# MetaFormer block on one core: gate weights spread by DMA, one PSUM bank for each expert of the last pair, and GpSimd taking two bands and seven additions

## The chip, the core and the metric

The kernel runs on 1 core of one Trainium2 chip. The metric is device time in microseconds (us); lower is better. The kernel before takes 136.04 us (median of 3 runs).

The engines are called as in the profile: PE (TensorE matmul) and PEld (its weight loads), DVE (VectorE), ACT (ScalarE), POOL (GpSimd), SP (SyncE, which issues most DMAs).

## What is computed

Eight images of 64 channels and 16x16 pixels go through a block of two halves, all in float32:

```python
x = x + conv_att(ln_c(x))          # first half
t = to_tokens(x)                   # (8, 256, 64)
t = t + ffn(ln_t(t))               # second half

# conv_att: qkv = 1x1 conv to 192 channels; dw = 5x5 depthwise; pw = grouped 1x1 (24 groups of 8);
#           ReLU linear attention over qkv and pw (16 heads of 8); 1x1 projection to 64; batch norm

def ffn(x, Wg, bg, W1, b1, W2, b2):            # 8 experts, hidden 256, top 2
    top_w, top_i = top_k(x @ Wg + bg, 2)
    w_dense = sum(one_hot(top_i) * softmax(top_w)[..., None])
    for e in range(8):
        h = gelu(x @ W1[e] + b1[e])
        out += w_dense[:, e:e + 1] * (h @ W2[e] + b2[e])
```

All eight experts are computed for every token; the gate weight `w_dense`, zero for six of them, multiplies the result.

## The kernel before, in words

The work is cut into `PAIRS` = 4 pairs `s` of images, each 2 x 256 tokens. Each engine runs one instruction list written out by hand; semaphores tie them together. There is no planner: the order in the program is the order on the engine. `mm` is a helper that records most matmuls, so most of them carry its line, L911; they are told apart by operands.

**Start.** PE makes the qkv products into PSUM; DVE and ACT scale them into `MS` (`scale_qkv`, `SCALED_V` = 6 on DVE, `SCALED_S` = 10 on ACT). Of the 24 convolution bands (`BAND`), DVE makes two of each head (L605), ACT the third (L413), and band number `ON_POOL` = 1 is made on POOL (L347). DVE then transposes head 0 (L667), for which all 16 scalings must be done, and PE starts the convolution: 24 bands of 5 matmuls.

**Middle.** For each pair: attention (`kv`, `qt`, `num`, `attt`, `proj`), a second layer norm, and `xt`, which turns the normalised tokens; ACT copies them to `XS` (`copy_xs`). `gate(part)` makes the gate logits of two pairs, DVE turns them into weights (`read_gates`, `gaps`, `places`, `softmax`).

**Experts.** `first_layer(s, e)`: two halves of two 128x512 matmuls each (high and low part of `W1`); each half goes to one of four PSUM banks 0, 1, 6, 7 and ACT applies GELU to it (L516). A bank can be written again when its GELU is done. `second_layer(s, e)` multiplies the hidden rows by `W2` (L1131) into `Y` banks 2 and 3, two experts to a bank. DVE weighs each result (`weigh`, L834: add `B2`, multiply by the weight `WB`, from PSUM into `WY`) and adds it up (`add_up`, L840) in `outs`. PE runs the second layers four at a time between blocks of first layers; the last eight, those of pair 3, stand in one row at the end.

**How a gate weight reaches all rows.** `tokens(s)` (L1086, L1089) turns the weights of a pair, split in two parts (`WDS`, made by DVE at L823 and L824), and the residual tokens `X2`; ACT copies both (`read_tokens`: `WT` L498, `outs` L499). Then `weights(s, ep)` spreads the weights of two experts over 128 rows with two matmuls against a 0/1 matrix `PICK`, and ACT copies the bank to `WB` (`read_weights`, L507). `MISC` = banks 5 and 4 alternate for this.

The PE order around the places that matter, word for word:

```python
            for e in range(QUAD):
                second_layer(0, e)
            xt(3)
            tokens(0)
            first_layer(0, 7)
            weights(0, 0)
            first_layer(1, 0)
```

`tokens(0)` waits there, through `wait_misc`, for ACT's copy of the tokens that `xt(3)` has just turned (`a_read[3]`, `A_XT`), since bank 4 holds them.

Of the kernel before, what the change touches and what calls it, by code (L numbers as in the profile page):

```python
# [48 lines left out]
C_ROWS = C_IOTA + E  # L49
C_END = C_ROWS + 2 * E  # L50
# [4 lines left out]
def constants():  # L55
# [11 lines left out]
    c[0:4 * E, C_ROWS:C_ROWS + 2 * E] = np.tile(np.eye(2 * E).reshape(2 * E, 2, E).transpose(0, 2, 1)  # L67
                                                 .reshape(2 * E, 2 * E), (2, 1))
# [11 lines left out]
def build(nc, x, w_qkv, w_dw, w_pw, w_proj, vectors, wg, w1, b1, w2, b2, consts, select, out):  # L80
    ctx = ExitStack()
    with ctx:
# [33 lines left out]
        PICK = sb("PICK", [128, E, 2, C], F32R)  # L116
        WT = sb("WT", [128, 2, N], F32R)
# [23 lines left out]
        WDS = sb("WDS", [128, PAIRS, 2, 2, 2, E])  # L141
# [53 lines left out]
        SCALED_V, SCALED_S = 6, 10  # L195
        ON_POOL = 1
# [4 lines left out]
        Y_BANKS, LAST_Y_BANK = (2, 3), 6  # L201
        MISC = (5, 4)
        GATE_BANKS = 1, 4
        MISC_GATES = (3,)
# [7 lines left out]
        warm_set, pick_set = sem("warm_set"), sem("pick_set")  # L212
# [24 lines left out]
        gap_ready, exp_ready, wds_ready, wt_read = sem("gap_ready"), sem("exp_ready"), sem("wds_ready"), sem("wt_read")  # L237
        misc_ready, misc_read = sem("misc_ready"), [sem("misc_read_0"), sem("misc_read_1")]
        h_ready, gelu_done, w2_done, y_read = sem("h_ready"), sem("gelu_done"), sem("w2_done"), sem("y_read")
        out_ready, stored = sem("out_ready"), sem("stored")  # L240
# [21 lines left out]
        def misc_use(s, k):  # L262

            n = (1 + E // 2) * s + k
            return n if n < MISC_GATES[0] else n + len(MISC_GATES)

        def reads_before(n):

            return sum(m % 2 == n % 2 and m not in MISC_GATES for m in range(n))

        def uses_before(n):

            return sum(m not in MISC_GATES for m in range(n))

# [18 lines left out]
        def y_bank(s, e):  # L293

            return LAST_Y_BANK if s == PAIRS - 1 and e == E - 1 else Y_BANKS[e // 2 % 2]

        def band_factors(g):

            return (band[:, g].rearrange("p d (x o) -> p (d x) o", o=I),
                    RS[:, g].rearrange("p d x -> p (d x)").unsqueeze(2).broadcast_to([128, DY * W, I]),  # L300
                    PW[:, g, :].unsqueeze(1).broadcast_to([128, DY * W, I]))

# [3 lines left out]
        def _(sp):  # L306
# [17 lines left out]
            for s in range(PAIRS):  # L324
                sp.wait_ge(out_ready, s + 1)
                sp.dma_start(out[2 * s:2 * s + 2].rearrange("b c y x -> (b c) (y x)"), outs[:, s, :]).then_inc(stored, 16)
            sp.wait_ge(stored, 16 * PAIRS)

        @block.gpsimd
        def _(pool):  # L330
# [6 lines left out]
            pool.memset(WT[:, :, :].bitcast(F32), 0.0).then_inc(pads_set, 1)  # L337
            pool.wait_ge(pads_set, 6)
# [8 lines left out]
            pool.tensor_tensor(*band_factors(ON_POOL), ALU.mult).then_inc(band_p, 1)  # L347
# [25 lines left out]

        @block.scalar
        def _(act):
# [23 lines left out]
            act.wait_ge(pads_set, 6)  # L399
# [4 lines left out]
            for j in range(6):  # L404
                scale_qkv(j, 1)
            for j in range(6, 8):
                for h in range(2):
                    scale_qkv(j, h)
# [83 lines left out]
            def read_tokens(s):  # L492

                n = misc_use(s, 0)
                act.wait_ge(misc_ready, uses_before(n) + 1)
                if s >= 2:
                    act.wait_ge(misc_ready, uses_before(misc_use(s - 1, 0)))
                act.activation(WT[0:4 * E, s % 2, :], PS[0:4 * E, MISC[n % 2], N:2 * N], ACT.Copy).then_inc(wt_read, 1)  # L498
                act.activation(outs[:, s, :], PS[:, MISC[n % 2], 0:N], ACT.Copy).then_inc(misc_read[n % 2], 1)  # L499

            def read_weights(s, ep):

                n = misc_use(s, 1 + ep)
                act.wait_ge(misc_ready, uses_before(n) + 1)
                if s >= 2:
                    act.wait_ge(y_read, E * (s - 2) + 2 * ep + 2)
                act.activation(WB[:, s % 2, 2 * ep:2 * ep + 2, :].rearrange("p e n -> p (e n)"),  # L507
                               PS[:, MISC[n % 2], :], ACT.Copy).then_inc(misc_read[n % 2], 1)

# [46 lines left out]
            high(3)  # L556
            copy_xs(3)
            read_tokens(0)
            gelu(0, 7)
            read_weights(0, 0)  # L560
            gelu(1, 0)
            read_weights(0, 1)
            gelu(1, 1)
            gelu(1, 2)
            read_weights(0, 2)
            gelu(1, 3)
            read_weights(0, 3)
            gelu(1, 4)
            read_tokens(1)
            gelu(1, 5)  # L570
            gelu(1, 6)
            read_weights(1, 0)
            gelu(1, 7)
            read_weights(1, 1)
            for s in (2, 3):
                gelu(s, 0)
                gelu(s, 1)
                read_weights(s - 1, 2)
                gelu(s, 2)
                read_weights(s - 1, 3)  # L580
                gelu(s, 3)
                read_tokens(s)
                if s == 2:
                    gelu(s, 4)
                    gelu(s, 5)
                    read_weights(s, 0)
                    gelu(s, 6)
                    read_weights(s, 1)
                    gelu(s, 7)
            for k in range(QUAD):  # L590
                gelu(PAIRS - 1, QUAD + k)
                read_weights(PAIRS - 1, k)

        @block.vector
        def _(dve):
# [68 lines left out]
            for h in range(8):  # L664
# [4 lines left out]
                else:  # L669
                    dve.transpose(qp[:, 3 * h:3 * h + 3], head(h)).then_inc(qp_ready, 1)  # L670
                if h > 0:
# [131 lines left out]
            def softmax(part):  # L803
# [13 lines left out]
                for b in range(2):  # L817
                    i = dve.tensor_tensor(WDN[:, pairs, :, b, :], O1.rearrange("p (s b h) e -> p b s h e", b=2, h=2)[:, b],
                                          O2.rearrange("p (s b h) e -> p b s h e", b=2, h=2)[:, b], ALU.add)
                link(i)  # L820
                whole = WDN[:, pairs].rearrange("p s h b e -> p (s h) (b e)")
                parts = WDS[:, pairs].rearrange("p s h k b e -> p k (s h) (b e)")
                link(dve.tensor_copy(parts[:, 0].bitcast(F32R), whole))  # L823
                dve.tensor_tensor(parts[:, 1].bitcast(F32R), whole, parts[:, 0], ALU.subtract).then_inc(wds_ready, 1)  # L824

            def combine(s, ep):

                for n in (misc_use(s, 0), misc_use(s, 1 + ep)):
                    dve.wait_ge(misc_read[n % 2], reads_before(n) + 1)
# [3 lines left out]
                def weigh(e):  # L833
                    dve.scalar_tensor_tensor(out=WY[:, e % 2, :], in0=PS[:, y_bank(s, e), N * (e % 2):N * (e % 2) + N],  # L834
# [11 lines left out]
                if y_bank(s, 2 * ep) == y_bank(s, 2 * ep + 1):  # L846
# [51 lines left out]
            combine(0, 0)  # L898
            read_gates(1)
            combine(0, 1)  # L900
            gaps(1)
            places(1)
            combine(0, 2)
            softmax(1)
            for n in range(3, PAIRS * E // 2):
# [3 lines left out]
        def _(pe):  # L909
# [143 lines left out]
            def gate(part):  # L1053
# [7 lines left out]
                for n in MISC_GATES if part == 1 else ():  # L1061
                    pe.wait_ge(misc_read[n % 2], reads_before(n))
# [7 lines left out]
            def wait_misc(n):  # L1070

                if n in (MISC_GATES[0] + 1, MISC_GATES[-1] + 1, MISC_GATES[-1] + 2) and n not in MISC_GATES:
                    pe.wait_ge(gate_read, 2)
                if n >= 2:
                    pe.wait_ge(misc_read[n % 2], reads_before(n))
                else:
                    pe.wait_ge(b_read[PAIRS - 1], B_PROJ)
                    pe.wait_ge(a_read[PAIRS - 1], A_XT)

            def tokens(s):  # L1080

                n = misc_use(s, 0)
# [177 lines left out]
```

## Time and profile before

| | us |
|---|---|
| runs (3) | 136.04 median, 135.68 to 136.23 |
| profiled execution | 136.38 |
| its span, first to last instruction | 134.6 |
| PE busy | 126.6 (94%) |
| ACT busy | 95.2 (71%) |
| DVE busy | 85.4 (63%) |
| POOL busy | 22.3 (17%) |

The profiled execution takes 1.78 us more than its span, and 0.34 us more than the median of the runs. The chain that ended last (followed back from the last instruction) is 90% PE, 4% DVE and 2% ACT.

### The profile page before, as it was taken

Reading aid. Unit: us, or ns where it says so; the run is one execution under the profiler, and the core shown is the slowest. Engines: PE = TensorE matmul, PEld = TensorE weight load, DVE = VectorE, ACT = ScalarE, POOL = GpSimd, SP = SyncE. Lnnn points to the kernel's source line nnn. Section 1 sums busy time; section 2 is a strip of 40 time slices with the busy share of each in tenths; the row PEclk is TensorE's granted clock in tenths of the full one; section 3 lists DMA queues with packets and bytes.
Section 4 is the critical chain, followed back from the end, with each engine's and each line's share of the span. In section 5 each row is a group of like instructions: output and inputs, shape, how many; then the busy total and the mean of one; then the engine's idle time right before and its main releaser. Section 6 shows DMA issues by size and latency. Waiting matters only on the chain.

```text
span 134.6 us, 2740 instructions
## 1 busy us (share of the span) xinstructions
PE 126.6 (94%) x954; PEld 102.9 (76%) x954; DVE 85.4 (63%) x252; ACT 95.2 (71%) x220; POOL 22.3 (17%) x22
## 2 busy tenths in 40 slices
PE   7999699999999999979999899999999999999970
PEld 7498699999998899957875786776867668677640
DVE  0528899999976986974693099946318072270793
ACT  3357999999984928359994797493984939759400
POOL 4005999300000000230720004000000000000000
PEclk9999999999999999999999999999999999999999
DMA  4779300000000000000000000010000100001001
GB/s 123 227 167 215 100 2 0 0 5 0 0 2 0 5 0 0 5 0 0 0 0 0 5 2 0 2 39 5 0 0 0 39 5 0 0 0 39 0 7 39
DMA packets 3655, 3.48 MB, mean 26 GB/s; under 512 B 978, under 2 KB 3258, under 8 KB 3642
## 3 DMA queue, kind: packets, MB, share of 16 engines
q1 hardware_dynamic: 3264, 3.09, 9.0%
q10 hardware_dynamic: 378, 0.22, 0.6%
q8 instruction: 8, 0.13, 0.4%
q14 instruction: 5, 0.04, 0.1%
HBM read 2.78 MB, written 0.52 MB: 25 GB/s over the span
## 4 chain that ended last, share of the span: by engine, by line
PE 90%; DVE 4%; ACT 2%; issue 2%; POOL 0%; DVEq 0%; ACTq 0%; POOLq 0%
PE PS L911 61%; PE PS L1131 20%; PE PS L1012 3%; PE PS L1049 2%; ACT MS L390 1%; PE PS L1018 1%; DVE SQ L834 1%; PE PS L1035 1%; DVE XP L840 1%; PE PS L1086 1%; PE PS L1089 1%; ACT KR L428 1%; DVE BAND L605 1%; ACT XS L490 0%; DVE MS L657 0%
## 5 line engine op out<-in xcount | busy, mean ns | idle before, releaser
L516 ACT ACTIVATE MS<-PS,B 128x512 f32<-128x512 f32 x48 | 30.1, 694 | 12.3 <-PE PS L911 12.2
L834 DVE SCALAR_TENSOR_TENSOR SQ<-PS,B,BAND 128x256 f32<-128x256 f32 x32 | 14.1, 479 | 28.6 <-ACT XP L499 10.1
L911 PE MATMUL PS<-QP,BAND 128*128 128x120 f32 (+2 forms) x240 | 27.0, 275 | 0.8 <-DVE QP L667 0.8
L911 PEld LDWEIGHTS PS<-QP,BAND 128*128 128x128 f32 x240 | 26.9, 192 | 1.0 <-issue 1.0
L911 PE MATMUL PS<-XS,W1H 128*128 128x512 f32 x64 | 26.7, 416 | 0.7 <-ACT XS L490 0.7
L911 PE MATMUL PS<-XS,W1L 128*128 128x512 f32 x64 | 25.3, 395 | 0.0
L1131 PE MATMUL PS<-MS,W 128*64 128x256 f32 x192 | 22.3, 383 | 0.0
L1131 PEld LDWEIGHTS PS<-MS,W 128*64 128x64 f32 x192 | 13.2, 137 | 7.4 <-issue 0.4
L413 ACT ACTIVATE BAND<-RS,PW 128x80 f32<-128x80 f32 x64 | 17.2, 434 | 0.0
L911 PEld LDWEIGHTS PS<-XS,W1H 128*128 128x128 f32 x64 | 12.1, 189 | 5.3 <-issue 2.1
L840 DVE TENSOR_TENSOR XP<-XP,SQ 128x256 f32<-128x256 f32 x32 | 13.4, 420 | 0.6
L911 PEld LDWEIGHTS PS<-XS,W1L 128*128 128x128 f32 x64 | 12.1, 189 | 1.6
L605 DVE TENSOR_TENSOR BAND<-RS,PW 128x640 f32<-128x640 f32 x15 | 11.6, 809 | 0.0
L360 POOL TENSOR_TENSOR SM<-SM,HALF 128x4 f32<-128x4 f32 x4 | 4.2, 1046 | 38.3 <-DVE SM L755 38.3
L516 ACT ACTIVATE BAND<-PS,B 128x512 f32<-128x512 f32 x16 | 10.2, 706 | 0.0
L507 ACT ACTIVATE BAND<-PS 128x512 f32<-128x512 f32 x16 | 9.8, 615 | 0.0
L1131 PE MATMUL PS<-BAND,W 128*64 128x256 f32 x64 | 7.6, 379 | 0.0
L911 PEld LDWEIGHTS PS<-WT,PICK 128*128 128x128 f32 x32 | 5.9, 188 | 1.5
L911 PE MATMUL PS<-WT,PICK 128*128 128x256 f32 x32 | 6.4, 282 | 0.0
L1131 PEld LDWEIGHTS PS<-BAND,W 128*64 128x64 f32 x64 | 4.6, 137 | 2.3
L670 DVE STREAM_TRANSPOSE QP<-MS 128x384 f32<-128x384 f32 x7 | 6.0, 859 | 0.0
L474 ACT ACTIVATE BAND<-PS 128x512 f32<-128x512 f32 x4 | 2.4, 606 | 5.0 <-PE PS L1035 5.0
(120 smaller groups left out, 172.6 us busy)
## 6 DMA issues: line engine op xcount, KB each, us to landing
W<-in_w_dram SPq DMA_DIRECT2D x3, 512.0 KB, 6.8
X<-in_x_dram SPq DMA_DIRECT2D x2, 256.0 KB, 3.2
out_dram<-XP SPq DMA_DIRECT2D x4, 128.0 KB, 1.7
VEC<-in_vectors_dram SPq DMA_DIRECT2D x1, 132.0 KB, 3.1
SELF<-in_select_dram ACTq DMA_DIRECT2D x1, 100.8 KB
WQ<-in_w_qkv_dram SPq DMA_DIRECT2D x2, 48.0 KB, 3.4
PW<-in_w_pw_dram SPq DMA_DIRECT2D x1, 96.0 KB, 3.1
CST<-in_consts_dram SPq DMA_DIRECT2D x1, 85.0 KB, 3.3
```

The source lines that it names most:

```text
L360: pool.tensor_tensor(SM[:, s, 1, :], SM[:, s, 0, :], HALF[:, 0:TILES], ALU.pow).then_inc(r2_ready, 1)
L413: i = act.activation(band[:, g].rearrange("p d (x o) -> p o (d x)", o=I)[:, o], RS[:, g].rearrange("p d x -> p (d x)"), ACT.Copy, scale=PW ...
L507: act.activation(WB[:, s % 2, 2 * ep:2 * ep + 2, :].rearrange("p e n -> p (e n)"), PS[:, MISC[n % 2], :], ACT.Copy).then_inc(misc_read[n % ...
L516: act.activation(hidden(n), PS[:, h_bank(n), :], ACT.Gelu, bias=B1[:, k:k + 1]).then_inc(gelu_done, 1)
L605: dve.tensor_tensor(*band_factors(g), ALU.mult).then_inc(band_v, 1)
L670: dve.transpose(qp[:, 3 * h:3 * h + 3], head(h)).then_inc(qp_ready, 1)
L834: dve.scalar_tensor_tensor(out=WY[:, e % 2, :], in0=PS[:, y_bank(s, e), N * (e % 2):N * (e % 2) + N], scalar=B2[:, e:e + 1], in1=WB[:, s % ...
L840: i = dve.tensor_tensor(outs[:, s, :], outs[:, s, :], WY[:, e % 2, :], ALU.add)
L911: return pe.matmul(PS[0:parts, bank, cols[0]:cols[1]], lhsT, rhs, start=start, stop=stop)
L1012: i = pe.matmul(PS[rows, CHAIN_BANK[s], 0:2 * KW], KR[:, s, r, rows], VM[:, s, half, r].rearrange("p b v -> p (b v)"), start=r == 0, stop= ...
L1049: i = pe.transpose(PS[:, CHAIN_BANK[s], 128 * t:128 * t + 128], XHL[:, s % 2, t].rearrange("p k c -> p (k c)"), IDT)
L1131: i = pe.matmul(PS[C * b:C * b + C, y_bank(s, e), N * (e % 2):N * (e % 2) + N], W2[:, KC * e + k, :], hidden(KC * (E * s + e) + k)[:, N * ...
```

## The change

It has four parts.

1. **Gate weights by transfers.** `PICK`, the 32 matmuls against it and ACT's 16 copies to `WB` go. ACT copies the turned weights to `WT` (16x256, no split in two parts), SP writes `WT` to a buffer in DRAM (`spread`), waits for that, and reads it back with four DMAs for each pair, each of 4 experts for 64 rows, 256 KB. DVE waits on `wb_in` for each four experts.
2. **Y banks.** Pairs 0 to 2 use banks 2, 3, 4 in turn, two experts to a bank. In the last pair each expert has its own bank (`LAST_Y_BANKS`). `tokens(s)` always uses bank 5.
3. **Adding.** In the last pair POOL adds up experts 0 to 6 in `outs`, DVE only weighs, and adds the last.
4. **Start.** POOL makes bands 0 and 1; the scalings are shared 8 and 8; DVE no longer makes band 0.

With these the hand-written orders change too: `tokens(0)` stands ahead of `xt(3)`; ACT reads the tokens of pair 1 after `gelu(1, 3)` instead of after `gelu(1, 4)`; DVE reads the second gates ahead of `combine(0, 0)` instead of behind it.

```diff
-        SCALED_V, SCALED_S = 6, 10
-        ON_POOL = 1
+        SCALED_V, SCALED_S = 8, 8
+        ON_POOL = 2
-        Y_BANKS, LAST_Y_BANK = (2, 3), 6
-        MISC = (5, 4)
+        Y_BANKS, LAST_Y_BANKS = (2, 3, 4), (2, 3, 4, 5, 0, 1, 6, 7)
+        TOKEN_BANK = 5
...
+            def spread_weights(s):
+                sp.wait_ge(wt_read, s + 1)
+                sp.dma_start(spread[s], WT[:, s % 2, :]).then_inc(wt_out, 16)
+                sp.wait_ge(wt_out, 16 * (s + 1))
+                if s >= 2:
+                    sp.wait_ge(y_read, E * (s - 1))
+                for quad in range(2):
+                    for b in range(2):
+                        rows = slice(E * b + QUAD * quad, E * b + QUAD * quad + QUAD)
+                        sp.dma_start(WB[C * b:C * b + C, s % 2, QUAD * quad:QUAD * quad + QUAD, :],
+                                     spread[s, rows, :].unsqueeze(0).broadcast_to([C, QUAD, N]))\
+                            .then_inc(wb_in[s % 2][quad], 16)
...
+            spread_weights(0)
+            spread_weights(1)
+            store(0)
+            spread_weights(2)
+            store(1)
+            spread_weights(3)
+            store(2)
+            store(3)
...
+            for g in range(ON_POOL):
+                pool.tensor_tensor(*band_factors(g), ALU.mult).then_inc(band_p, 1)
...
+            s = PAIRS - 1
+            pool.wait_ge(tokens_read, PAIRS)
+            for e in range(E - 1):
+                pool.wait_ge(y_read, E * s + e + 1)
+                if e >= 1:
+                    pool.wait_ge(added, e)
+                pool.tensor_tensor(outs[:, s, :], outs[:, s, :], WY[:, e % 2, :], ALU.add).then_inc(added, 1)
...
-            copy_xs(3)
             read_tokens(0)
+            copy_xs(3)
             gelu(0, 7)
...
+            for e in range(4):
+                gelu(1, e)
             read_tokens(1)
+            for e in range(4, E):
+                gelu(1, e)
...
+                dve.wait_ge(wb_in[s % 2][2 * ep // QUAD], 32 * (s // 2 + 1))
...
                     for e in range(2 * ep, 2 * ep + 2):
                         dve.wait_ge(w2_done, E * s + e + 1)
+                        if e >= 2:
+                            dve.wait_ge(added, e - 1)
                         weigh(e)
-                        add_up(e)
+                    if ep == E // 2 - 1:
+                        dve.wait_ge(added, E - 1)
+                        add_up(E - 1)
...
             def second_layer(s, e):
                 pe.wait_ge(gelu_done, KC * (E * s + e) + KC)
-                if E * s + e >= 4:
-                    pe.wait_ge(y_read, E * s + 2 * (e // 2) - 2)
+                bank, at, end = y_part(s, e)
+                if s == PAIRS - 1:
+                    if bank in Y_BANKS:
+                        pe.wait_ge(y_read, E * s - 4 + 2 * Y_BANKS.index(bank))
+                    elif bank == TOKEN_BANK:
+                        pe.wait_ge(tokens_read, PAIRS)
+                    else:
+                        pe.wait_ge(gelu_done, KC * E * PAIRS - 4 + H_MANY.index(bank) + 1)
+                elif E * s + e >= 6:
+                    pe.wait_ge(y_read, E * s + 2 * (e // 2) - 4)
+                elif e >= 4:
+                    pe.wait_ge(gate_read, 2)
```

How the order moves on PE, right behind the second layers of pair 0's first four experts (the first row of each piece; CST,BAND x4 is `xt(3)`, the pair of x2 rows is `tokens(0)`, the W1H and W1L rows are first layers). Before:

```order
L1131 MATMUL PS<-MS,W 64x256 x16
L1049 MATMUL PS<-CST,BAND 128x128 x4
L1086 MATMUL PS<-CST,WDS 32x128 x2
L1089 MATMUL PS<-CST,BAND 128x128 x2
L911 MATMUL PS<-XS,W1H 128x512
L911 MATMUL PS<-XS,W1L 128x512
L911 MATMUL PS<-XS,W1H 128x512
L911 MATMUL PS<-XS,W1L 128x512
L911 MATMUL PS<-WT,PICK 128x256 x2
```

And in the changed kernel (its line numbers are its own):

```order
L1096 MATMUL PS<-MS,W 64x256 x16
L1052 MATMUL PS<-CST,WDN 16x128 x2
L1055 MATMUL PS<-CST,BAND 128x128 x2
L1025 MATMUL PS<-CST,BAND 128x128 x4
L887 MATMUL PS<-XS,W1H 128x512
L887 MATMUL PS<-XS,W1L 128x512
L887 MATMUL PS<-XS,W1H 128x512
L887 MATMUL PS<-XS,W1L 128x512
L887 MATMUL PS<-XS,W1H 128x512
```

`tokens(0)` has moved ahead of `xt(3)`, and the two matmuls against `PICK` behind each first layer are gone.

On ACT, around the tokens of pair 1 (MS,B and BAND,B rows of L516 are GELUs, two to an expert; L507 is `read_weights`, L498 and L499 are `read_tokens(1)`). Before:

```order
L507 ACTIVATE BAND<-PS 128x512
L516 ACTIVATE MS<-PS,B 128x512 x2
L507 ACTIVATE BAND<-PS 128x512
L516 ACTIVATE MS<-PS,B 128x512 x2
L498 ACTIVATE WT<-PS 32x256
L499 ACTIVATE XP<-PS 128x256
L516 ACTIVATE MS<-PS,B 128x512 x2
```

In the changed kernel, where L515 is the GELU and L506 and L507 are `read_tokens`:

```order
L515 ACTIVATE BAND<-PS,B 128x512 x2
L515 ACTIVATE MS<-PS,B 128x512 x8
L506 ACTIVATE WT<-PS 16x256
L507 ACTIVATE XP<-PS 128x256
L515 ACTIVATE MS<-PS,B 128x512 x4
L515 ACTIVATE BAND<-PS,B 128x512 x4
```

The GELUs of expert 4 of pair 1 stood ahead of the two token copies and now stand behind them; the copies to `WB` are gone.

On DVE, the last rows of the program, pair 3 (SQ is `weigh`, XP is `add_up`). Before:

```order
L834 SCALAR_TENSOR_TENSOR SQ<-PS,B,BAND 128x256 x2
L840 TENSOR_TENSOR XP<-XP,SQ 128x256 x2
L834 SCALAR_TENSOR_TENSOR SQ<-PS,B,BAND 128x256
L840 TENSOR_TENSOR XP<-XP,SQ 128x256
L834 SCALAR_TENSOR_TENSOR SQ<-PS,B,BAND 128x256
L840 TENSOR_TENSOR XP<-XP,SQ 128x256
```

In the changed kernel, the last of pair 2 and then pair 3:

```order
L807 SCALAR_TENSOR_TENSOR SQ<-PS,B,BAND 128x256 x2
L813 TENSOR_TENSOR XP<-XP,SQ 128x256 x2
L807 SCALAR_TENSOR_TENSOR SQ<-PS,B,BAND 128x256 x2
L813 TENSOR_TENSOR XP<-XP,SQ 128x256 x2
L807 SCALAR_TENSOR_TENSOR SQ<-PS,B,BAND 128x256 x8
L813 TENSOR_TENSOR XP<-XP,SQ 128x256
```

Eight weighings now follow each other with one addition behind them; the seven others stand on POOL.

## Rows read from the trace of the kernel before

**Rows 1.** The page, parts 1 and 2: busy us; granted clock in tenths.

```profile
PE 126.6 (94%) x954; PEld 102.9 (76%) x954; DVE 85.4 (63%) x252; ACT 95.2 (71%) x220; POOL 22.3 (17%) x22
...
PEclk9999999999999999999999999999999999999999
```

**Rows 2.** The chain that ended last, start of the convolution: start us, us, what.

```profile
14.35 0.62 issue
...
15.63 25.92 PE PS L911 x230
```

**Rows 3.** Timelines of DVE, ACT and POOL up to 28 us: start us, us.

```profile
11.57 2.04 DVE L632 TENSOR_SCALAR MS<-PS,R 128x192 f32<-128x192 f32 x6
27.99 0.18 DVE L681 TENSOR_TENSOR INV<-INV,VEC 128x64 f32<-128x64 f32 x1
11.63 3.25 ACT L390 ACTIVATE MS<-PS,R 128x192 f32<-128x192 f32 x10 [0.79 <-PE PS L911]
11.57 1.29 POOL L347 TENSOR_TENSOR BAND<-RS,PW 128x640 f32<-128x640 f32 x1 [4.36 <-DVE RS L636]
12.82 0.38 POOL L350 TENSOR_SCALAR INV<-VEC 128x64 f32<-128x64 f32 x1
18.71 5.94 POOL L354 TENSOR_TENSOR INV<-INV,HALF 128x32 f32<-128x32 f32 x1
```

**Rows 4.** The chain that ended last: around `tokens(0)`; a block of four first layers.

```profile
73.69 0.73 issue
...
75.02 6.49 PE PS L911 x36
...
102.00 4.41 PE PS L911 x20
```

**Rows 5.** Timeline of PE in the last first layers.

```profile
119.44 0.40 PE L911 MATMUL PS<-WT,PICK 128*128 128x256 f32 x2
...
119.67 0.40 PE L911 MATMUL PS<-XS,W1H 128*128 128x512 f32 x1
...
119.91 0.40 PE L911 MATMUL PS<-XS,W1L 128*128 128x512 f32 x1
```

**Rows 6.** Timeline of ACT: token copies, and a block of four GELUs.

```profile
75.06 0.37 ACT L498 ACTIVATE WT<-PS 32x256 fp32r<-32x256 f32 x1 [0.73 <-PE PS L1089]
...
75.60 1.23 ACT L516 ACTIVATE BAND<-PS,B 128x512 f32<-128x512 f32 x2
...
102.70 2.43 ACT L516 ACTIVATE MS<-PS,B 128x512 f32<-128x512 f32 x4 [2.30 <-PE PS L911]
105.00 0.62 ACT L507 ACTIVATE BAND<-PS 128x512 f32<-128x512 f32 x1
```

**Rows 7.** Timeline of DVE: second gates, `gaps(1)` up to `combine(0, 2)`.

```profile
79.22 0.22 DVE L778 TENSOR_TENSOR BAND<-PS,VEC 128x64 f32<-128x64 f32 x1
...
81.44 0.65 DVE L787 MAX8 BAND<-BAND 128x8 f32<-128x8 f32 x8
...
83.83 0.88 DVE L834 SCALAR_TENSOR_TENSOR SQ<-PS,B,BAND 128x256 f32<-128x256 f32 x2
```

**Rows 8.** Timelines of PE and DVE at the end.

```profile
128.51 1.90 PE L1131 MATMUL PS<-BAND,W 128*64 128x256 f32 x16
...
131.51 0.48 DVE L834 SCALAR_TENSOR_TENSOR SQ<-PS,B,BAND 128x256 f32<-128x256 f32 x1
132.03 0.42 DVE L840 TENSOR_TENSOR XP<-XP,SQ 128x256 f32<-128x256 f32 x1
```

**Rows 9.** DMA: issue of X on SP, its readers on DVE, landing of the stores.

```profile
0.72 0.38 SPq L307 DMA_DIRECT2D X<-in_x_dram  x1
...
3.72 0.60 DVE L610 COPY XP<-X 128x512 f32<-128x512 f32 x1 [3.72 <-DMA X<-in_x_dram]
4.62 0.61 DVE L610 COPY XP<-X 128x512 f32<-128x512 f32 x1 [0.30 <-DMA X<-in_x_dram]
...
out_dram<-XP SPq DMA_DIRECT2D x4, 128.0 KB, 1.7
```

More of the change, by code:

```diff
@@ L260, in head @@
             return MS[:, :, :].rearrange("p j (q h i) -> p h q j i", q=3, i=I)[:, h]
[L262 to L273, printed above, removed]
         def h_bank(n):
@@ L291, in masked_v, with y_part @@
                     PAR[:, b:b + 1])
-        def y_bank(s, e):
-            return LAST_Y_BANK if s == PAIRS - 1 and e == E - 1 else Y_BANKS[e // 2 % 2]
+        def y_part(s, e):
+            bank, at = (LAST_Y_BANKS[e], 0) if s == PAIRS - 1 else (Y_BANKS[(E * s + e) // 2 % 3], N * (e % 2))
+            return bank, at, at + N
         def band_factors(g):
@@ L403, in _ @@
             act.wait_ge(r1_ready, 1)
-            for j in range(6):
+            for j in range(SCALED_S):
                 scale_qkv(j, 1)
-            for j in range(6, 8):
-                for h in range(2):
-                    scale_qkv(j, h)
             def bands(g):
@@ L897, in _ @@
             dve.wait_ge(b2_in, 32)
-            combine(0, 0)
             read_gates(1)
-            combine(0, 1)
             gaps(1)
             places(1)
-            combine(0, 2)
+            combine(0, 0)
+            combine(0, 1)
             softmax(1)
-            for n in range(3, PAIRS * E // 2):
+            for n in range(2, PAIRS * E // 2):
                 combine(*divmod(n, E // 2))
@@ L1068, in gate, with tokens @@
                 i.then_inc(gate_ready, 1)
[L1070 to L1075, printed above, removed]
-                else:
[L1077 to L1082, printed above, removed]
-                wait_misc(n)
-                pe.wait_ge(wds_ready, s // OF_PART + 1)
+            def tokens(s):
+                if s == 0:
+                    pe.wait_ge(b_read[PAIRS - 1], B_PROJ)
+                else:
+                    pe.wait_ge(tokens_read, s)
+                pe.wait_ge(wdn_ready, 2 * (s // OF_PART) + 2)
                 for half in range(2):
-                    pe.transpose(PS[0:4 * E, MISC[n % 2], N + 128 * half:N + 128 * half + 128],
-                                 WDS[:, s, half].rearrange("p k b e -> p (k b e)"), IDT)
+                    pe.transpose(PS[0:2 * E, TOKEN_BANK, N + 128 * half:N + 128 * half + 128],
+                                 WDN[:, s, half].rearrange("p b e -> p (b e)"), IDT)
                 for half in range(2):
-                    i = pe.transpose(PS[:, MISC[n % 2], 128 * half:128 * half + 128],
+                    i = pe.transpose(PS[:, TOKEN_BANK, 128 * half:128 * half + 128],
                                      X2[:, 2 * s + half].rearrange("p b c -> p (b c)"), IDT)
-                i.then_inc(misc_ready, 1)
-            def weights(s, ep):
-                n = misc_use(s, 1 + ep)
-                wait_misc(n)
-                pe.wait_ge(wt_read, s + 1)
-                pe.wait_ge(pick_set, 1)
-                for e in range(2):
-                    i = mm(MISC[n % 2], (N * e, N * e + N), PICK[:, 2 * ep + e].rearrange("p b c -> p (b c)"),
-                           WT[:, s % 2, :], True, True)
-                i.then_inc(misc_ready, 1)
+                i.then_inc(turned, 1)
             def first_layer(s, e):
@@ L1122, in second_layer @@
                 pe.wait_ge(gelu_done, KC * (E * s + e) + KC)
[L1123 to L1124 removed]
+                bank, at, end = y_part(s, e)
+                if s == PAIRS - 1:
[9 more added lines that the diff above has]
+                    pe.wait_ge(gate_read, 2)
                 else:
@@ L1130, in second_layer @@
                 for k, b in ((0, 0), (0, 1), (1, 1), (1, 0)):
-                    i = pe.matmul(PS[C * b:C * b + C, y_bank(s, e), N * (e % 2):N * (e % 2) + N],
+                    i = pe.matmul(PS[C * b:C * b + C, bank, at:end],
                                   W2[:, KC * e + k, :], hidden(KC * (E * s + e) + k)[:, N * b:N * b + N],
@@ L1171, in _ @@
                 second_layer(0, e)
+            tokens(0)
             xt(3)
-            tokens(0)
             first_layer(0, 7)
-            weights(0, 0)
             first_layer(1, 0)
-            weights(0, 1)
-            first_layer(1, 1)
             gate(1)
-            first_layer(1, 2)
-            weights(0, 2)
-            first_layer(1, 3)
-            weights(0, 3)
+            for e in range(1, QUAD):
+                first_layer(1, e)
             for e in range(QUAD, E):
@@ L1187, in _ @@
             tokens(1)
-            first_layer(1, 5)
-            first_layer(1, 6)
-            weights(1, 0)
-            first_layer(1, 7)
-            weights(1, 1)
+            for e in range(5, E):
+                first_layer(1, e)
             for e in range(QUAD):
@@ L1197, in _ @@
                 first_layer(s, 1)
-                weights(s - 1, 2)
+                tokens(s)
                 first_layer(s, 2)
-                weights(s - 1, 3)
                 first_layer(s, 3)
-                tokens(s)
                 for e in range(QUAD, E):
                     second_layer(s - 1, e)
+                for e in range(QUAD, E):
+                    first_layer(s, e)
                 if s == 2:
-                    first_layer(s, 4)
-                    first_layer(s, 5)
-                    weights(s, 0)
-                    first_layer(s, 6)
-                    weights(s, 1)
-                    first_layer(s, 7)
                     for e in range(QUAD):
                         second_layer(s, e)
-            for k in range(QUAD):
-                first_layer(PAIRS - 1, QUAD + k)
-                weights(PAIRS - 1, k)
             for e in range(E):
```

120 lines of the change are left out of this document (34 added, 86 removed).

## The prediction

> **What bounds the kernel now.** I read the page first: PE is busy 94% of the span and its granted clock is full in every slice [rows 1]. Then the chain that ended last, in order of time: it lies on PE but for three places. One is the start, where PE waits for the first transpose on DVE, and DVE in turn waited 0.62 us with nothing of its own to do [rows 2]; ACT's ten scalings end at 11.63 + 3.25 = 14.88, DVE's six at 13.61, so it waited for ACT [rows 3]. The second is a hole of 0.73 us in front of `tokens(0)` [rows 4], which waits for ACT's copy of the tokens just turned. The third is the tail on DVE: PE ends at 128.51 + 1.90 = 130.41, DVE at 132.03 + 0.42 = 132.45 [rows 8]. So an instruction taken off PE is worth its pitch, one taken off ACT or DVE nothing in itself.
>
> **The change part by part.** Call the end of PE's last matmul P; all times are on the clock of the span before.
>
> *Start.* DVE's six scalings take 2.04, a pitch of 0.33; eight end at about 11.57 + 2.04 + 0.66 = 14.27. ACT's ten give a pitch of 0.31, eight end near 14.25 [rows 3]. The transposes then start near 14.4 instead of 14.97 (14.35 + 0.62 [rows 2]). POOL's two bands of 1.29 end at 12.86 and 14.15 [rows 3], ahead of the first matmul; POOL reads and writes other tiles than the scalings do, as band 1 did before. The convolution follows without a gap for 25.92 us [rows 2], so its start moves everything: **-0.6**. Hidden: POOL's powers end at 24.65 + 1.3 = 25.9, ahead of their first reader at 27.99 - 0.6 = 27.4 [rows 3]. Were DVE to slow POOL's second band by half, PE would reach it (a band later, 1.08 us by 25.92 / 24) still in time.
>
> *`tokens(0)` ahead of `xt(3)`.* It no longer uses bank 4, so it doesn't wait for ACT's copy; that copy is next needed by `gate(1)`, two first layers on (1.9 us), and it takes ACT about 0.5. The way to 75.02 [rows 4] loses the 0.73 and perhaps 0.15 of the restart: **-0.8** (0.7 to 0.9).
>
> *The 32 `PICK` matmuls.* Two of them start at 119.44 and the next first-layer matmul at 119.67 [rows 5]: 0.234 a pair (their listed durations overlap), 16 pairs: **-3.75**. What could hide this gain is ACT, whose GELUs free the banks. Its pitch is (105.00 - 102.70) / 4 = 0.575 [rows 6] against PE's 2 x 0.235 = 0.47 a half [rows 5]. In a block of eight halves the first GELU starts 0.70 after the block (102.70 [rows 6] against 102.00 [rows 4]), the fourth ends at 0.70 + 2.30 + 0.1 = 3.1, and PE wants its bank at 7 x 0.47 = 3.3: no stall, by 0.2. Between blocks lie 3.6 us of second layers, and ACT catches up, the more so since it lost 16 copies.
>
> *ACT reads the tokens of pair 1 ahead of `gelu(1, 4)`.* Here a new wait arises. Count from the start of `first_layer(1, 4)`. PE needs 0.94 for it, 0.6 for `tokens(1)` (75.02 less 73.69 + 0.73 [rows 4]); ACT then copies for 75.60 - 75.06 = 0.54 [rows 6] and starts the first GELU at about 2.15, where before it ran ahead of the copies. GELU k ends at 2.15 + 0.1 + 0.575 (k + 1). PE wants the bank of the first GELU at 0.94 + 0.6 + 0.94 = 2.5, has it at 2.85, and that of the fourth at 4.6 instead of 3.9: **+0.75**, once. Pairs 2 and 3 read their tokens behind `gelu(s, 1)`, when PE has long turned them. Bounds 0 and 0.9.
>
> *Transfers.* Nobody waits for them if they land in time; the first pair is the tightest. `WT` is there at 75.06 + 0.37 = 75.43 [rows 6]; it comes 0.6 earlier by the start, 0.73 by the hole and 0.6 because `xt(3)`, four transposes like `tokens(0)`, now stands behind: 73.5. A store of 128 KB lands 1.7 after issue; X's first 256 KB are there 3.72 - 0.72 = 3.0 after issue and the next 0.9 later [rows 9]. So the first four experts (512 KB) land at 73.5 + 1.7 + 3.9 + 0.1 = 79.2, the other four at 81.0. `first_layer(0, 7)` starts at 75.02 - 0.6 - 0.8 = 73.6; it, the next and `gate(1)` (6.49 less five experts of 0.94 and four pairs of 0.234 [rows 4, 5]: 0.85) end near 76.3, and DVE is through with second gates, gaps and places 0.5 (two instructions of 0.22) + (83.83 - 81.44) = 2.9 later [rows 7], at 79.3. So `combine(0, 0)` starts at 79.3 and its two weighings end at 80.2 (0.88 [rows 7]). PE needs them for bank 2 at `second_layer(0, 6)`: the block starts at 75.02 + 6.49 = 81.51 less 0.6, 0.8 and four `PICK` pairs (0.94), 79.15, and its third expert 1.8 later, at 80.95. Slack 0.7: **0**. Later pairs have it easier: the weights of pair 1 land about 6 us ahead of the bank that would stop PE, those of pair 3 some 3 us ahead of the first weighing. SP's stores stand behind transfers, but each waits for sums that are complete before the next weights are wanted.
>
> [...]
>
> *Tail.* Before, DVE spends 0.94 on each expert (weigh and add), more than PE's 0.9, and ends at P + 2.04. Now weigh 7 starts at P + 0.1 and ends at P + 0.58. The addition 6 on POOL: its weighing ends at P - 0.32; a 128x64 instruction of POOL takes 0.38 and one of 128x640 1.29 [rows 3], on the line between them 128x256 is 0.68, with both as bounds; it ends at P + 0.46, DVE's last addition at P + 1.05: **-1.0**. POOL's pitch of 0.68 + 0.1 stays under PE's 0.9, so no queue forms. The separate banks take PE's waits for weighings away, of which it had none in this stretch, and the store behind the last addition is as before.
>
> [...]
>
> **Sum.** -0.6 - 0.8 - 3.75 + 0.75 - 1.0 = -5.4. The profiled execution took 136.38, so its like would take 131.0; the median of the runs lies 0.34 lower, which gives 130.7.
>
> **The rivals.**
> - *A, the sum as it stands*: 130.7; chance 0.60.
> - *B, the first weights come late.* For: a DRAM buffer is written and then read by 64 rows at once, which nothing in this trace does; the slack is 0.7. Against: X moves at 0.9 a 256 KB beside other loads. At half that rate the first four land at 81.0, and PE stands 1.0: 131.7, up to 132.5 if the write takes 0.8 longer too. Chance 0.15.
> - *C, POOL's additions queue.* The first weighing ends at P - 5.7; seven additions of pitch p, then DVE's, end at P - 5.1 + 7p. From p = 0.9 on they lengthen the tail, at 1.02 all of its gain is gone (131.7), at 1.29, the upper bound, + 0.1 it would be 134.3. For: POOL's start behind a semaphore isn't shown at this pace. Against: the line between two rows. Chance 0.10.
> - *D, the wait at pair 1's tokens doesn't arise*, since a GELU slips in or PE's halves are slower: 130.0. Chance 0.08.
> - *E, slower than before.* One mechanism: the weights of pair 0 land so late that PE loses 5.4 at `second_layer(0, 6)`. That needs them at 79.2 + 0.7 + 5.4 = 85.3 or later, 11.8 after `WT` where I count 5.7, as would be if 64 rows reading the same 4 KB went one after another (about 50 GB/s). With every pair hit the same way the time would be 137 or more. Against: the wide loads of constants at the start come from one row of DRAM too and hold nobody up. Chance 0.04, and 0.03 for a loss between B and this that ends within 0.5% of before.
>
> **Range and chances.** A measurement of this kernel tells about 0.5% from no change. A to D reach from 130.0 to 132.5; with 0.2 for the spread of the runs below, the range is 129.8 to 132.4. Faster 0.94, same 0.02, slower 0.04.
>
> **What would show each step.** The first convolution matmul near 15.05. No hole in front of `tokens(0)`. Blocks of four first layers of 3.75 to 3.95 us. A hole of 0.4 in front of `first_layer(1, 6)`, and short ones after it. DVE's first weighing near 79.3, held by places and not by a DMA. POOL's seven additions 0.9 apart, 0.7 each; DVE's last addition 1.05 behind PE's last matmul. Wrong if PE waits at `second_layer(0, 6)` for DVE, if the additions run closer than 0.9 to their own length, or if the GELUs' pitch grows and holds every block.

## The result

The changed kernel takes 131.15 us (median of 4 runs, 130.39 to 136.53), the kernel before 136.11 (median of 4). In some executions of every kernel here the time is some microseconds longer at a mean granted clock near 0.97; the ratios and, but where a mean clock is given, the times below leave them out, and four of the profiles (tokens0_behind_xt3, more_room, two_late, more_room_two_late) are such ones, with PE's granted clock at 0.50 from about 10 to 17 us and the convolution starting near 18.8 instead of 15, so that only stretches behind that point are read there. The ratio is 0.962 (95% interval 0.957 to 0.968): 5.1 us faster.

The profiled execution took 131.66 (136.38 before), its span is 129.8. The page of the changed kernel, parts 1, 2 and 6 (busy us; granted clock; DMAs with KB and us to landing):

```profile
PE 123.1 (95%) x922; PEld 98.2 (76%) x922; DVE 81.9 (63%) x242; ACT 85.8 (66%) x201; POOL 27.7 (21%) x29
...
PEclk9999999999999999999999999999999999999998
...
BAND<-spread_dram SPq DMA_DIRECT2D x16, 256.0 KB, 4.7
```

PE is as full as before [rows 1] over a shorter span, and the granted clock held (0.995 in the mean, 1.00 up to 128 us, behind PE's last matmul). The chain that ended last, of the changed kernel, beside [rows 2, 4]:

```profile
15.02 25.92 PE PS L887 x230
...
72.47 0.32 PE PS L1052 x2
72.78 0.22 PE PS L1055 x2
73.00 0.44 PE PS L1025 x4
73.44 5.56 PE PS L887 x28
79.00 1.88 PE PS L1096 x16
80.88 0.12 issue
81.00 1.95 PE PS L1096 x16
82.94 1.12 PE PS L887 x4
...
85.08 0.67 ACT MS L515
85.75 0.14 issue
85.89 2.35 PE PS L887 x8
88.24 3.60 PE PS L1096 x32
...
99.79 3.92 PE PS L887 x16
...
119.17 2.77 PE PS L1096 x23
```

The hole of 0.73 [rows 4] is gone; a block of four first layers takes 3.92 where it took 4.41. Two waits remain among the experts: a short one at 80.9, and one where the chain leaves PE for ACT's GELU up to 85.75. The timelines of DVE, SP and ACT in the changed kernel show what they are:

```profile
79.97 0.88 DVE L807 SCALAR_TENSOR_TENSOR SQ<-PS,B,BAND 128x256 f32<-128x256 f32 x2 [0.90 <-DMA BAND<-spread_dram]
...
73.44 0.35 SPq L312 DMA_DIRECT2D spread_dram<-WT  x1
74.89 2.38 SPq L319 DMA_DIRECT2D BAND<-spread_dram  x4
...
84.82 0.36 ACT L507 ACTIVATE XP<-PS 128x256 f32<-128x256 f32 x1
85.08 2.37 ACT L515 ACTIVATE MS<-PS,B 128x512 f32<-128x512 f32 x4
```

DVE had been through with its places at 79.07 and waited 0.90 for the transfer. ACT's GELUs of expert 4 of pair 1 start at 85.08, behind the token copies, and PE goes on behind the first of them. And the timelines at the end, beside [rows 8]:

```profile
120.97 5.95 POOL L388 TENSOR_TENSOR XP<-XP,SQ 128x256 f32<-128x256 f32 x7 [41.68 <-DVE SQ L807]
...
124.33 1.90 PE L1096 MATMUL PS<-BAND,W 128*64 128x256 f32 x16
...
126.28 0.48 DVE L807 SCALAR_TENSOR_TENSOR SQ<-PS,B,BAND 128x256 f32<-128x256 f32 x1 [0.21 <-PE PS L1096]
126.95 0.42 DVE L813 TENSOR_TENSOR XP<-XP,SQ 128x256 f32<-128x256 f32 x1 [0.18 <-POOL XP L388]
```

PE ends at 126.23, DVE at 127.37, 1.14 behind it instead of 2.04; the last 0.18 of DVE's wait is for POOL.

### The profile page after: what moved, and what is told of

Same layout as the page of the kernel before. It is cut to its first block, busy times and chain, and to the rows that moved or that the text cites. A ratio compares the mean times of both kernels' runs of the same rounds, so it can differ in the third digit from the quotient of the medians.

```text
span 129.8 us, 2655 instructions
## 1 busy us (share of the span) xinstructions
PE 123.1 (95%) x922; PEld 98.2 (76%) x922; DVE 81.9 (63%) x242; ACT 85.8 (66%) x201; POOL 27.7 (21%) x29
## 4 chain that ended last, share of the span: by engine, by line
PE 86%; DVE 3%; DMA 3%; POOL 2%; ACT 2%; issue 1%; POOLq 1%; DVEq 0%; ACTq 0%
PE PS L887 57%; PE PS L1096 19%; PE PS L988 3%; DMA CST<-in_consts_dram 3%; POOL XP L388 2%; DVE MS L608 2%; PE PS L994 1%; PE PS L1025 1%; PE PS L1011 1%; PE PS L947 1%; PE PS L1052 1%; PE PS L1055 1%; POOLq L79 1%; ACT KR L437 1%; ACT MS L515 1%
## 5 line engine op out<-in xcount | busy, mean ns | idle before, releaser
L515 ACT ACTIVATE MS<-PS,B 128x512 f32<-128x512 f32 x48 | 29.2, 681 | 12.0 <-PE PS L887 12.0
L388 POOL TENSOR_TENSOR XP<-XP,SQ 128x256 f32<-128x256 f32 x7 | 5.1, 727 | 42.5 <-DVE SQ L807 41.7
L813 DVE TENSOR_TENSOR XP<-XP,SQ 128x256 f32<-128x256 f32 x25 | 10.5, 420 | 0.6 <-POOL XP L388 0.2
L581 DVE TENSOR_TENSOR BAND<-RS,PW 128x640 f32<-128x640 f32 x14 | 10.7, 801 | 0.0
L515 ACT ACTIVATE BAND<-PS,B 128x512 f32<-128x512 f32 x16 | 9.8, 695 | 0.0
L483 ACT ACTIVATE BAND<-PS 128x512 f32<-128x512 f32 x4 | 2.4, 604 | 5.0 <-PE PS L1011 5.0
L506 ACT ACTIVATE WT<-PS 16x256 f32<-16x256 f32 x4 | 1.5, 365 | 6.1 <-PE PS L1055 6.1
L360 POOL TENSOR_TENSOR INV<-INV,HALF 128x32 f32<-128x32 f32 x1 | 5.5, 5457 | 0.1
```

The lines of the kernel that those rows point to most:

```text
L360: pool.tensor_tensor(INV[:, 1, 0:C // 2], INV[:, 0, 0:C // 2], HALF[:, 0:C // 2], ALU.pow).then_inc(inv_ready, 1)
L388: pool.tensor_tensor(outs[:, s, :], outs[:, s, :], WY[:, e % 2, :], ALU.add).then_inc(added, 1)
L515: act.activation(hidden(n), PS[:, h_bank(n), :], ACT.Gelu, bias=B1[:, k:k + 1]).then_inc(gelu_done, 1)
L581: dve.tensor_tensor(*band_factors(g), ALU.mult).then_inc(band_v, 1)
L813: i = dve.tensor_tensor(outs[:, s, :], outs[:, s, :], WY[:, e % 2, :], ALU.add)
```

## The experiments

All kernels are edits of the changed kernel, and their times are compared with those of after_again, its repetition. Two stretches of PE are read in each trace: from the first row of `second_layer(0, 4)` to the first of `second_layer(0, 6)`, 1.78 us where nothing is waited for, and from there to `second_layer(1, 0)`.

**after_again.** No edit. 

> The changed kernel once more, as the measure for the three beside it. 130.4 to 131.2 us; PE's last matmul 1.1 to 1.2 us ahead of DVE's last addition.

Measured 130.81 to 131.50 (130.81, 130.92, 130.95, 131.50); ratio to before 0.9645 (0.962 to 0.967). Stretches 1.93 and 7.17; DVE ends 1.15 behind PE. The wait for the first weights was 0.15 here, 0.29 in the profile above (2.07).

**tail_on_dve.**

```diff
-                        if e >= 2:
-                            dve.wait_ge(added, e - 1)
                         weigh(e)
-                    if ep == E // 2 - 1:
-                        dve.wait_ge(added, E - 1)
-                        add_up(E - 1)
+                        add_up(e)
```

POOL's seven additions are left out. 

> The changed kernel with POOL's seven additions back on DVE (own banks kept). Theory (POOL takes 0.42 us an expert off DVE, which is slower than PE by 0.04 to 0.1 us an expert): DVE ends about 2.0 us behind PE's last matmul instead of 1.14, so 0.8 to 0.9 us slower than the changed kernel. Rival (the separate banks bring the gain, POOL's pitch of 0.87 us eats its own): within 0.3 us of the changed kernel.

Measured 131.25, 132.39, 132.48 (two at a mean clock of 0.992); these times alone don't tell 0.3 from 0.8, the trace does. Its chain that ended last:

```profile
118.23 7.09 PE PS L1085 x63
...
126.84 0.42 DVE XP L806
```

PE's last matmul ends at 125.29, DVE at 127.26: 1.97 behind, where it is 1.15 in after_again. The theory holds: the last pair's own banks alone bring 0.07 at the tail (2.04 before), POOL brings 0.82. The first stretch is 1.78 in this trace: here PE did not wait for the first weights at all, though nothing in that part was edited.

**tokens1_behind_gelu4.**

```diff
-            for e in range(4):
+            for e in range(5):
                 gelu(1, e)
             read_tokens(1)
-            for e in range(4, E):
+            for e in range(5, E):
                 gelu(1, e)
```

> ACT reads the tokens of pair 1 behind the GELUs of expert 4 instead of ahead of them. Theory: the hole in front of first_layer(1, 6) and the short ones after it go, 0.6 to 0.75 us faster than the changed kernel, and the weights of pair 1 land 1 us later, which nobody waits for at the end. Rival: the hole moves to a later wait (the weights of pair 1 come later) and the time stays within 0.2 us.

Measured 130.59, 131.42, 131.66. The chain that ended last in its trace:

```profile
79.90 0.89 DVE SQ L807 x2
80.78 0.14 issue
80.92 1.95 PE PS L1096 x16
82.87 1.12 PE PS L887 x4
83.99 0.22 PE PS L1052 x2
84.20 0.22 PE PS L1055 x2
84.42 2.83 PE PS L887 x12
87.25 3.60 PE PS L1096 x32
```

The three first layers behind the tokens run without a break, and the second stretch is 6.26 instead of 7.17: the hole of 0.9 is gone, as the theory has it. The first stretch, ahead of the edit, was 2.29, a wait of 0.51 for the first weights. The times of the runs alone don't decide; two ran at a mean clock of 0.987.

**tokens0_behind_xt3.** `xt(3)` ahead of `tokens(0)`, which waits for `a_read[3]`, and `copy_xs(3)` ahead of `read_tokens(0)`.

```diff
+            xt(3)
             tokens(0)
-            xt(3)
             first_layer(0, 7)
```

> tokens(0) back behind xt(3) with its wait for the copied tokens, ACT's order as before. Theory: PE stands 0.7 us there, and the first weights come 0.7 + 0.6 us later, so the weighings that PE wants at second_layer(0, 6) end 0.6 us later against PE's own schedule and add up to 0.6 us there: 0.8 to 1.4 us slower than the changed kernel. Rival (another wait hides behind it): within 0.3 us.

Measured 133.84, 133.99, 134.49: 3.0 slower than the changed kernel, more than twice what was expected. The order's own hole is there as computed (0.73 of idle ahead of `tokens(0)`). The rest is at the first weights; PE and SP in its trace, and the stretch from 88 to 90 us (columns as in the table of transfers_late below):

```profile
87.49 2.86 PE L1097 MATMUL PS<-BAND,W 128*64 128x256 f32 x16 [2.02 <-DVE SQ L807]
...
78.48 0.35 SPq L312 DMA_DIRECT2D spread_dram<-WT  x1
80.91 2.38 SPq L319 DMA_DIRECT2D BAND<-spread_dram  x4
...
88.00:90.00 2.00, 2.00 (x14) 1.18 (x10) 1.90 (x6) 0.00 (x0) 0.00 (x0) 0.59 0.00 0
```

The first stretch is 3.96, a wait of 2.18, and the 16 matmuls behind it took 2.86 instead of 1.90, at a granted clock of 0.59. The wait adds up from the traces: 0.29 as in the changed kernel; 0.44, since SP starts the write 5.05 ahead of `second_layer(0, 4)` instead of 5.49, which is the order's part; 0.98, since the write of `WT` took 2.43 from issue to the next issue instead of 1.45; and 0.48, since the first weighing came 5.56 behind the first read's issue instead of 5.08. The three timed runs had a mean clock of 0.998 to 1.000, so they did not pay for the clock; whether they had so slow a write is not shown, though their 3.0 need a wait near 2 us there.

**start_as_before.** `SCALED_V, SCALED_S = 6, 10`, `ON_POOL = 1`, band 0 on DVE, as in the kernel before. 

> The changed kernel with the start of before: scalings 6 and 10, band 0 on DVE, band 1 alone on POOL. Theory: the convolution starts at 15.6 instead of 15.0 on the clock of the span, 0.6 us slower than the changed kernel (131.3 to 131.7). Rival: a later wait absorbs it, within 0.2 us.

Measured 131.76, 131.82 (against 130.81 to 131.50). From DVE's first scaling to the convolution 4.10 (11.05 to 15.15) against 3.44 (10.93 to 14.37) in after_again: 0.66, and nothing absorbs it; the runs are 0.74 slower in the mean.

**no_transfers.** POOL fills `WB` with 0.125 once the convolution is done; SP spreads nothing.

```diff
+            pool.wait_ge(conv_moved, 9)
+            pool.memset(WB[:, :, :, :].rearrange("p s e n -> p (s e n)"), 0.125).then_inc(wb_set, 1)
-                dve.wait_ge(wb_in[s % 2][2 * ep // QUAD], 32 * (s // 2 + 1))
+                dve.wait_ge(wb_set, 1)
```

> The gate weights are left out: POOL fills WB once with a constant, SP moves nothing between the experts (the sums are therefore not the reference's). Theory (transfers are hidden but for the first pair): 0.1 to 0.3 us faster than the changed kernel, the wait at second_layer(0, 6) gone. Rival (the traffic slows engines or the stores): 0.5 us faster or more, with shorter matmuls, GELUs or a faster last store.

Measured 130.79, 131.07, 131.11, 131.12; the changed kernel 130.81 to 131.50. First stretch 1.78, second 7.15 as with transfers. So 4 MB of traffic costs PE its wait for the first weights and nothing else that shows in the time; GELUs (681 and 682 ns in the mean) and first-layer matmuls (422 and 423 ns for W1H) keep their lengths. The stores do not: their median from issue to landing is 2.3 in the changed kernel (1.8 to 3.1 in its edits with transfers) and 1.7 without, as before. The first three are waited for by nobody, and the span ends 2.4 behind DVE's last addition in both traces.

**transfers_late.** Four transfers of 256 KB ahead of pair 0's, into the slot that pair 1 uses later.

```diff
+                if s == 0:
+                    for n in range(4):
+                        sp.dma_start(WB[C * (n % 2):C * (n % 2) + C, 1, 4 * (n // 2):4 * (n // 2) + 4, :],
+                                     spread[0, 0:QUAD, :].unsqueeze(0).broadcast_to([C, QUAD, N])).then_inc(idle_in, 16)
+                if s == 1:
+                    sp.wait_ge(idle_in, 16 * 4)
```

> Four idle transfers of 256 KB ahead of the four of pair 0. Theory (slack at second_layer(0, 6) is used up): at about 1.15 us each the first weights land 4.6 us later and PE stands there 4.5 us: 4 to 4.8 us slower than the changed kernel, near 135.2. Rival (there is slack of a microsecond or more, or DVE catches up ahead of PE): under 3.5 us slower.

Measured 138.28, 138.56, 139.78, 139.93: 8 slower, where 4 to 4.8 were expected. PE in its trace, and the table by stretch (busy us of PE, PEld, DVE, ACT, POOL, then granted clock, DMA share, GB/s):

```profile
86.94 3.68 PE L1103 MATMUL PS<-BAND,W 128*64 128x256 f32 x16 [5.61 <-DVE SQ L814]
...
82.00:84.00 2.00, 0.00 (x0) 0.00 (x0) 0.00 (x0) 0.00 (x0) 0.00 (x0) 1.00 1.04 234
84.00:86.00 2.00, 0.00 (x0) 0.00 (x0) 0.09 (x1) 0.00 (x0) 0.00 (x0) 0.72 0.75 166
86.00:88.00 2.00, 1.06 (x6) 0.78 (x8) 1.93 (x5) 0.00 (x0) 0.00 (x0) 0.50 0.03 10
88.00:90.00 2.00, 2.00 (x14) 1.17 (x10) 1.83 (x8) 0.00 (x0) 0.00 (x0) 0.50 0.00 0
90.00:92.00 2.00, 2.00 (x8) 1.18 (x5) 1.93 (x8) 0.00 (x0) 0.00 (x0) 0.57 0.00 0
```

The hole is 5.8. The granted clock fell inside it, near 84.9 by the 0.72 of that row, and was at 0.50 until near 91.7 by the 0.57 of the last one: the 16 matmuls took 3.68 instead of 1.90. So there was no slack, as the theory says, and a long hole has a second price. Each idle transfer moved the first weights by 1.4 (first issue to first weighing 10.57 against 5.08).

**dead_matmuls.** 14 pairs of 128x256 matmuls that nobody reads, into bank 4; pairs 0 to 2 use banks 2 and 3 alone.

```diff
+                if (s == 1 and e >= 2) or (s > 1 and e % 2 == 1):
+                    pe.wait_ge(gate_read, 2)
+                    for c in range(2):
+                        mm(4, (N * c, N * c + N), W1H[:, 0:128], XS[:, 0, 0:N], True, True)
```

> The changed kernel with 14 pairs of 128x256 matmuls into bank 4, which nobody reads, behind first layers of pairs 1 to 3 (Y banks 2 and 3 alone for pairs 0 to 2, so that bank 4 is free). Theory (PE's pitch is the price of the PICK matmuls): 14 x 0.234 = 3.3 us slower than the changed kernel, less what falls into the hole behind tokens(1) (up to 0.4), and 0 to 1.7 us more if bank 2 is now waited for at second_layer(0, 4): 2.9 to 5.0. Rival (ACT bounds the blocks and hides matmuls): under 2 us.

Measured 135.10, 135.27, 135.69, 135.83 and two more up to 136.44; ratio to before 0.998 (0.995 to 1.002). From the start of the convolution to pair 3's second layers 108.03 against 103.97 in after_again: 4.06 more. 3.28 would be the pitch of 14 pairs; bank 2 made `second_layer(0, 4)` wait for the weighings (80.49, 1.36 late beyond the two pairs ahead of it), the wait behind it fell from 0.15 to nothing (first stretch 1.74), and 0.47 fell into the hole behind `tokens(1)` (second stretch 7.64 with its four pairs, where 7.17 + 0.94 = 8.11 would be). 3.28 + 1.36 - 0.19 - 0.47 = 3.98 of the 4.06. So a pair of such matmuls costs PE its pitch, ACT hides none but in that hole, and the third bank is worth 1.2 while the weights come by DMA.

**more_room.** The edit of tokens1_behind_gelu4, and:

```diff
-            for e in range(1, QUAD):
+            for e in range(1, QUAD + 1):
                 first_layer(1, e)
             for e in range(QUAD, E):
                 second_layer(0, e)
-            first_layer(1, 4)
             tokens(1)
```

> The changed kernel with first_layer(1, 4) moved ahead of second_layer(0, 4..7), so that PE comes to second_layer(0, 6) 0.94 us later, and the tokens of pair 1 read behind the GELUs of expert 4. Theory (two holes are left in the changed kernel: 0.15 to 0.35 us at second_layer(0, 6) and 0.75 behind tokens(1)): both go, 0.9 to 1.1 us faster than the changed kernel, 129.8 to 130.0. Rival (the holes move on): within 0.3 us.

Measured 129.57, 129.83, 129.91, 130.23; ratio to before 0.9553 (0.953 to 0.958), against 0.9645 (0.962 to 0.967) of after_again: 1.2 us faster than the changed kernel, the fastest here. Chain in its trace:

```profile
83.75 3.60 PE PS L1096 x32
87.36 0.32 PE PS L1052 x2
87.67 0.22 PE PS L1055 x2
87.89 2.81 PE PS L887 x12
90.70 3.60 PE PS L1096 x32
```

The four second layers take 3.60 and the three first layers 2.81, without a break; both holes are gone.

**two_late, more_room_two_late.** Two idle transfers instead of four, in the changed kernel and in more_room.

> Two idle transfers of 256 KB ahead of pair 0's four. Four of them made a hole of 5.6 us, 1.4 each, and the granted clock was half behind it. Theory (hole by the weights, and a price on top when the hole is long): a hole of 2.8 to 3.1 us at second_layer(0, 6), and the second layers behind it longer than 1.90 us for 16 if the clock falls: 3 to 5 us slower than the changed kernel. Rival (nothing but the hole): 2.8 to 3.1 us slower.

Measured eight from 135.58 to 137.34, 136.5 in the mean, at mean clocks of 0.969 to 0.987: 5.4 slower than the changed kernel, a little above the 3 to 5 expected. The hole is 3.5 (first stretch 5.30), the 16 matmuls behind it took 2.90. The theory holds; the hole is longer than expected since each transfer took 1.6 (first issue to first weighing 8.32).

> more_room with the same two idle transfers. Theory: PE comes 0.94 us later to the same wait, the hole is 1.9 to 2.2 us, and the clock may hold: 2 to 2.5 us slower than more_room. Rival (the clock falls at this length too): over 3 us slower than more_room.

One run took 132.32 at a mean clock of 1.000, 2.4 slower than more_room; three at a clock of 0.984 took 134.42 to 135.06, two at 0.96 took 138.22 and 138.52. The profile, one of the last two, has a hole of 2.6, with 3.29 for the 16 behind it. So the clock held in one execution and fell in others; whether their holes had the same length is not shown, and the theory and its rival are not decided.

**hole_alone.** no_transfers with the order of tokens0_behind_xt3. 

> The gate weights are left out as in no_transfers (WB a constant), and tokens(0) stands behind xt(3) again. Theory: this order costs its own hole of 0.7 to 0.9 us against no_transfers (131.0), so 131.7 to 131.9, and the rest of what tokens0_behind_xt3 lost (133.8 against 130.9) came from later weights. Rival: the order alone costs 2 us or more.

Measured 131.34, 131.78, 132.09, 132.71, 0.96 above no_transfers in the mean. Its PE timeline has the hole, and the 16 matmuls of `second_layer(0, 6)` on time:

```profile
73.70 0.38 PE L1051 MATMUL PS<-CST,WDN 128*16 128x128 f32 x2 [0.73 <-issue]
...
81.56 1.90 PE L1095 MATMUL PS<-BAND,W 128*64 128x256 f32 x16
```

The order alone costs 0.9 to 1.0; without transfers the other 2 us of tokens0_behind_xt3 are gone, so they came with the later weights.

## Why the prediction was right

The forecast was 5.4 us less, a time of 130.7; measured are 5.1 less by the ratio, a median of 131.15, and 4.7 less between the two profiled executions (136.38 to 131.66). The mechanisms were right, and the terms came out close, not exact: the misses are of up to 0.3 each, most of them to the slow side. The chain of the sum, with what each term measured in the two profiles:

| step | predicted | measured |
|---|---|---|
| start of the convolution | -0.6 | -0.61 (15.63 to 15.02); alone 0.66 |
| `tokens(0)` ahead of `xt(3)` | -0.8 | -0.95 (the way to `first_layer(0, 7)`: 1.92 to 0.97); alone 0.9 |
| `PICK` matmuls | -3.75 | not read alone; with the next two rows -2.60 |
| wait behind `tokens(1)` | +0.75 | +0.91 (7.17 against 6.26); gone with the order turned |
| first weights | 0 | +0.29 here; 0 to 0.5 in the other traces with this order |
| tail | -1.0 | -0.90; POOL's part alone 0.82 |
| last store to the end | 0 | +0.3 (2.1 to 2.5) |
| sum | -5.4 | -4.8 (span 134.6 to 129.8) |

Terms three to five together: from `first_layer(0, 7)` to pair 3's second layers PE took 48.33 before and 45.73 now, -2.60, where -3.75 + 0.91 + 0.29 gives -2.55. The term behind `tokens(1)` was somewhat small: its own working gives 4.6 - 3.9 = 0.7, not 0.75, and PE had the first bank 2.95 behind the start of `first_layer(1, 4)` instead of 2.85 (82.94 to 85.89). The change lies where rival A put it. The other rivals:

- *B, late weights.* It came in part, 0.29 where B had 1.0, and this is the term that was mis-sized. I counted 1.7 for the write and 3.9 for the first 512 KB; measured were 1.45 and 5.08. The 512 KB are two transfers, each 0.6 of issue on SP, and a further transfer over 64 rows moved the weights by 1.4 to 1.6, not X's 0.9. So the first weighing began at 79.97 instead of 79.3, PE was due at 80.71 (79.00 and two experts) instead of 80.95, and of the 0.7 of slack a wait of 0.29 was left. At about the same busy share of the DMA engines the first loads, mostly X over 128 rows, moved 315 GB/s (2 to 4 us of before, share 0.98) and the transfers over 64 rows 234 (82 to 84 us of transfers_late, share 1.04). That the number of rows is the cause is not shown: no run has the transfer with 128 rows, and the source, 4 KB read by 64 rows, differs too.
- *C, POOL's additions.* 5.95 us for seven, 0.73 each by the page, and 0.87 from one to the next (0.74 and 0.13 between, in the chain), where I had 0.68 and 0.10. It stayed under the 0.9 at which a queue begins, by 0.03, and cost 0.1. The 0.68 was read off a line between two different operations of POOL, so that it came so near was partly luck. Against DVE's 0.42 for the same addition, POOL's 0.73 is 1.7 times as long.
- *D* is excluded: the second stretch is 7.13 to 7.17 in each trace that has the order and a granted clock of 1.00 there, but for dead_matmuls, and 6.26 with the order turned.
- *E* needed the weights at 85.3. transfers_late brought the first weighing to 85.9, with a loss of 8, not 5.4: behind so long a hole the granted clock was 0.50 and added its own loss (3.68 us for 16 matmuls instead of 1.90), which E's working left out. Its decision point was therefore too late: two_late, with a hole of 3.5, is already as slow as the kernel before (ratio 1.002, 0.998 to 1.006).

What stays open: the last store, 2.1 to 2.5 from DVE's end to the span's end in the traces here with no pattern by kernel, so that the +0.3 is no effect of the change that these runs show; and the slow write in tokens0_behind_xt3. It is not the only one: of the 44 writes of `WT` in the traces 40 take 1.4 to 1.5 up to the next issue, and four, in three executions, 2.2 to 3.3. Only the one of 2.43 stood ahead of weights that PE was short of. That DVE reads the second gates ahead of `combine(0, 0)` was not tried alone.

## What to carry to other kernels

Work taken off the bounding engine is worth its pitch only if the wait that its removal exposes is moved too: two orders by hand (when ACT reads tokens, what PE does ahead of the first bank that needs the new weights) were worth 1.2 us after the large change had brought 5. A round trip through DRAM of 16 KB out and 512 KB in takes 6.3 to 6.8 us here and took 8.0 once; give it slack beyond that by what its lateness would cost. And price a hole on PE by its length: the short ones here (0.15 to 0.9 us, granted clock 1.00) cost themselves, the ones of 3.5 and 5.8 us the clock behind them too (0.50).

## What the runs showed of the hardware

- The granted clock of PE was 1.00 through holes of 0.15 to 0.9 us. In the four profiles with holes of 2.2, 2.6, 3.5 and 5.8 us it was 0.50 for 2 us or more behind them, and the 16 matmuls behind them took 2.86, 3.29, 2.90 and 3.68 us instead of 1.90. The first two lengths are not sure to cost it: the timed runs of tokens0_behind_xt3 (mean clock 0.998 to 1.000) and one of more_room_two_late (1.000) did not lose it.
- GpSimd's 128x256 float32 addition took 0.73 us (DVE's 0.42), and 0.87 from start to start when each waits for the one before and for a weighing.
- 4 MB of DMA traffic, up to 241 GB/s in a slice of the page, changed the mean lengths beside it by 1 ns at most (GELUs 681 against 682 without it, W1H matmuls 422 against 423, weighings 480 and 480); the stores took 2.3 us in the median to land instead of 1.7.
- A write of 16 KB to DRAM took 1.4 to 1.5 us up to the next issue in 40 of 44 cases, and 2.2 to 3.3 in four.
